# Feature columns transposed two at a time in a recommendation tower, and a last duo in which four late features are worked apart from the others

## What is computed

```python
e = jnp.stack([tbl_f[ids[:, f]] for f in range(26)], axis=1)
combined = jnp.concatenate([dense_output[:, None, :], e], axis=1)       # B, 27, 128
interactions = jnp.einsum('bfd,bgd->bfg', combined, combined)
z = jnp.concatenate([dense_output, interactions[:, iu, ju]], axis=1)    # iu, ju: upper triangle, k=1
h = jnp.concatenate([z, r_dense_output], axis=1)
h = jnp.maximum(h @ W_top1 + b_top1, 0.0)     # 607 -> 512
h = jnp.maximum(h @ W_top2 + b_top2, 0.0)     # 512 -> 256
y = h @ W_top3                                # 256 -> 1
```

## Time and profile before

| what | value |
|---|---|
| runs | median 523.08 us of 3 (521.77 to 524.66) |
| the profiled execution | 513.81 us, of which the span of its instructions is 512.0 us |
| granted TensorE clock, mean | 0.917 of full speed |
| PE busy | 408.9 us, 4352 matmul instructions |
| DVE, ACT, POOL busy | 245.8, 136.1 and 263.1 us |

### The profile page before, as it was taken

The page is one execution under the profiler, slowest core; times in us unless marked ns, Lnnn a source line. Parts: engine busy times, 40 slices in busy tenths (PEclk is TensorE's granted clock), DMA queues, the critical chain, the costliest instruction groups (busy, mean ns, idle before and its releaser), DMA issues.

```text
span 512.0 us, 10047 instructions
## 1 busy us (share of the span) xinstructions
PE 408.9 (80%) x4352; PEld 362.6 (71%) x4352; DVE 245.8 (48%) x312; ACT 136.1 (27%) x356; POOL 263.1 (51%) x280
## 2 busy tenths in 40 slices
PE   2885387857979688879878799797887968887998
PEld 2664366746867578768867678686776857886976
DVE  5994127554445454446453454545543454433332
ACT  2451112321223222223212322233212222123531
POOL 6787464552556636454635646264463654635000
PEclk9997596978999799998989979898998979989999
DMA  7978112221212212221212212123121221211000
GB/s 197 249 187 258 36 47 67 70 67 42 63 42 86 84 33 65 61 87 49 68 43 72 73 53 68 37 83 83 49 57 52 70 65 49 57 32 53 3 12 1
DMA packets 20133, 36.74 MB, mean 72 GB/s; under 512 B 6157, under 2 KB 9877, under 8 KB 20090
## 3 DMA queue, kind: packets, MB, share of 16 engines
q0 software_dynamic: 8704, 17.84, 12.7%
q1 hardware_dynamic: 5338, 9.08, 6.8%
q10 hardware_dynamic: 6048, 9.18, 5.9%
HBM read 36.07 MB, written 0.01 MB: 70 GB/s over the span
## 4 chain that ended last, share of the span: by engine, by line
PE 61%; another core or an unknown queue 13%; issue 12%; DVE 10%; ACT 2%; DMA 1%; SPq 0%; ACTq 0%; DVEq 0%
PE psB L382 23%; PE psG L408 14%; DVE one_hot L646 7%; PE psB L453 7%; PE psB L366 5%; PE psB L460 4%; PE psB L418 2%; PE psB L447 2%; DVE tab_lo L651 2%; PE psB L432 2%; DMA ET<-tbl 1%; PE psB L465 1%; DVE ZH L510 1%; ACT ET L553 1%
## 5 line engine op out<-in xcount | busy, mean ns | idle before, releaser
L307 POOL DMA_INDIRECT E<-tbl,gidx x272 | 262.3, 964 | 206.7 <-PE psB L366 109.7
L646 DVE TENSOR_TENSOR one_hot<-oidx,psR 125x1024 fp32r<-125x1024 int32 (+1 forms) x152 | 179.2, 1189 | 116.3 <-remote 60.4
L382 PE MATMUL psB<-one_hot,tab_hi 125*128 125x256 f32 x592 | 117.9, 321 | 19.0 <-ACT tab_hi L535 9.4
L408 PE MATMUL psG<-ET 128*52 128x52 f32 x2048 | 81.9, 228 | 44.4 <-issue 35.7
L382 PE MATMUL psB<-one_hot,tab_lo 125*128 125x256 f32 x592 | 105.4, 302 | 5.6 <-issue 4.7
L408 PEld LDWEIGHTS psG<-ET 128*52 128x52 f32 x2048 | 67.8, 139 | 59.2 <-issue 54.5
L382 PEld LDWEIGHTS psB<-one_hot,tab_hi 125*128 125x128 f32 x592 | 88.4, 206 | 27.3 <-issue 20.5
L382 PEld LDWEIGHTS psB<-one_hot,tab_lo 125*128 125x128 f32 x592 | 90.1, 208 | 9.1 <-issue 7.5
L669 DVE COPY_PREDICATED S<-second,psG 116x208 f32<-116x208 int32 x64 | 25.0, 391 | 103.1 <-ACT S L582 94.0
L582 ACT COPY S<-psG 116x208 f32<-116x208 f32 x64 | 21.2, 333 | 146.6 <-remote 82.0
L553 ACT COPY ET<-psB 128x512 f32<-128x512 f32 (+3 forms) x80 | 44.3, 572 | 50.9 <-PE psB L366 30.9
(11 more groups left out here) (46 smaller groups left out, 188.7 us busy)
## 6 DMA issues: line engine op xcount, KB each, us to landing
oidx<-hot_idx ACTq DMA_DIRECT2D x28, 256.0 KB
E<-tbl,gidx POOLq DMA_INDIRECT x272
ET<-tbl SPq DMA_DIRECT2D x3, 448.0 KB
oidx<-hot_idx SPq DMA_DIRECT2D x4, 256.0 KB
dense<-dense_pairs SPq DMA_DIRECT2D x8, 128.0 KB
ZH<-tbl SPq DMA_DIRECT2D x2, 448.0 KB
S<-tbl SPq DMA_DIRECT2D x2, 448.0 KB
oidx<-hot_idx ACTq DMA_DIRECT2D x7, 128.0 KB
```

The costliest lines, as they stand in the source:

```text
L307: nc.gpsimd.indirect_dma_start(E[:, n % SLOTS, i, :], None, gathered[feature_and_tile(n, i)[0]], bass.IndirectOffsetOnAxis(ap=gidx[:, 4 * ...
L382: product = nc.tensor.matmul(bank[:, t % 2 * DUO:(t % 2 + 1) * DUO], tab[0:ROWS_P, TABLE_BASE[t] + k0 + i, :], one_hot[0:ROWS_P, m % RING, ...
L408: gram = nc.tensor.matmul(psG[g % 2][q * LANE:q * LANE + M, a * M:(a + 1) * M], two[:, 0:M], two[:, PAIR:], start=True, stop=True)
L646: nc.vector.tensor_tensor(one_hot[0:ROWS_P, m % RING, 0:many], ids, rows, ALU.is_equal).then_inc(hot_full[m % RING], 1)
```

## The change

- Column transposes: `S` is laid out [.., duo parity, feature, 64], so that two neighbouring features lie side by side, and one transpose turns both: 13 for each duo, in four `C` steps (0 to 3, 4 to 7, 8 to 10 and 11 to 12 of the 13 twos) instead of 26 in seven. The even feature of a two lands on partitions 0 to 63, the odd one on 64 to 127.
- `U` has 128 partitions and 4 x 256 values. The first 128 columns (twos 0 to 10 but for two 5) hold both sides. The other 128 hold two 5 and the last two twos, one side in the first 64 columns on the lower partitions, the other in the last 64 on the upper ones; the rest stays zero. It is cleared once, in half 2.
- The splits are two: split 0 is four transposes of [128, 128]; split 1 is four float32 matmuls of `U` with `stacked`, two identity matrices one above the other, which brings the two halves together. ACT and DVE make high and low parts of 512 and of 256 values.
- The order of features becomes small tables first, gathered ones last, and the rows of W1 are permuted with it on the host.
- The last duo: T67 brings the last four features of the last tile. Its grams for that tile leave them out (44 columns instead of 52). A new step `late` computes them for all 32 sample groups (64 float32 matmuls with 8 moving columns) into one `psG` bank. The steps of half 16 are: gram, gram, last part of duo 6, gram, gram, C0, C1, C2, T67, split 0, late, first 0, C3, first 1, split 1, first 2, first 3, parts. `first` is the dense products and the first two thirds of the pairs of a first-layer block; its part then has only the last 3 products. In half 15 the order is grams, T64, parts, T65, parts 2 to 5 of duo 6, T66.

```diff
+    LATE = 4
+    TWOS = (F - 1) // 2
+    EARLY = TWOS - LATE // 2
+    COLUMNS = [range(t, min(t + 4, EARLY)) for t in range(0, EARLY, 4)] + [range(EARLY, TWOS)]
+    FIRST_BLOCKS = [(0, 1), (1, 2), (2, 4), (4, 5), (6, 8), (8, 10), (10, 11)]
+    LAST_BLOCKS = [(11, 13), (5, 6)]
...
-            rest = parts(DUOS - 2)[M1:]
-            return (rest[:1] + grams[:2] + rest[1:2] + grams[2:] + rest[2:] + columns(DUOS - 1) +
-                    splits(DUOS - 1) + parts(DUOS - 1))
+            d, turned = DUOS - 1, columns(DUOS - 1)
+            return (grams[:2] + parts(d - 1)[-1:] + grams[2:] + turned[:-1] + [("T", T_GROUPS - 1)] +
+                    splits(d)[:1] + [("late", d)] + firsts(d)[:1] + turned[-1:] + firsts(d)[1:2] + splits(d)[1:] +
+                    firsts(d)[2:] + parts(d))
...
+        if h == TILES - 1:
+            return spread(turns[:-2], steps + after) + parts(d - 1)[M1:-1] + turns[-2:-1]
...
-        S = sb("S", [P, F - 1, 2, DUO_J], f32)
+        S = sb("S", [P, 2, F - 1, DUO_J], f32)
...
-                        gram = nc.tensor.matmul(psG[g % 2][q * LANE:q * LANE + M, a * M:(a + 1) * M],
-                                                two[:, 0:M], two[:, PAIR:], start=True, stop=True)
+                        gram = nc.tensor.matmul(psG[g % 2][q * LANE:q * LANE + many, a * many:(a + 1) * many],
+                                                two[:, 0:many], two[:, PAIR:PAIR + many], start=True, stop=True)
...
+            def late_fill(d):
+                g, tile, many = LATE_FILL, 2 * d + 1, PAIR * LATE
+                wait_out(pe, ("T", T_GROUPS - 1))
+                pe.wait_ge(G_out[g % 2], g // 2)
+                for j in range(TILE_J):
+                    for q in range(GROUP // PAIR):
+                        two = ET[:, tile % ET_RING, j, q].rearrange("p f s -> p (f s)")
+                        gram = nc.tensor.matmul(psG[g % 2][q * LANE:q * LANE + M, j * many:(j + 1) * many],
+                                                two[:, 0:M], two[:, PAIR * F - many:], start=True, stop=True)
                 gram.then_inc(G_full[g % 2], 1)
...
+                if d == DUOS - 1 and b == len(COLUMNS) - 1:
+                    pe.wait_ge(G_out[LATE_FILL % 2], LATE_FILL // 2 + 1)
                 bank, full = wait_empty(pe, ("C", d, b))
-                for i, c in enumerate(COLUMNS[b]):
-                    turned = nc.tensor.transpose(bank[0:DUO_J, i * P:i * P + MT], S[0:MT, c - 1, d % 2, :],
-                                                 ident[0:MT, 0:MT])
+                for i, t in enumerate(COLUMNS[b]):
+                    two = S[0:MT, d % 2, 2 * t:2 * t + 2, :].rearrange("p f j -> p (f j)")
+                    turned = nc.tensor.transpose(bank[:, i * P:i * P + MT], two, ident[0:MT, 0:MT])
...
-            def turn_pairs(d, kp):
-                if kp == 0:
-                    last = {}
-                    for b in range(len(COLUMNS)):
-                        bank, used, _ = PLACE["C", d, b]
-                        last[bank] = used + 1
-                    for bank, count in last.items():
-                        pe.wait_ge(bank_out[bank], count)
+            def turn_pairs(d, i):
+                last = {}
+                for b in range(len(COLUMNS))[:-1] if i == 0 else range(len(COLUMNS))[-1:]:
+                    bank, used, _ = PLACE["C", d, b]
+                    last[bank] = used + 1
+                for bank, count in last.items():
+                    pe.wait_ge(bank_out[bank], count)
+                bank, full = wait_empty(pe, ("split", d, i))
                 for v in range(GROUP):
-                    turned = nc.tensor.transpose(bank[:, v * DUO_J:(v + 1) * DUO_J],
-                                                 U[0:DUO_J, v, kp * P:(kp + 1) * P], ident[0:DUO_J, 0:DUO_J])
+                    if i == 0:
+                        turned = nc.tensor.transpose(bank[:, v * P:(v + 1) * P], U[:, v, 0:P], ident[:, :])
+                        continue
+                    turned = nc.tensor.matmul(bank[:, v * DUO_J:(v + 1) * DUO_J], U[:, v, P:], stacked[:, :],
+                                              start=True, stop=True)
...
+            def copy(sides, low, high, base):
+                at, n = low - COLUMNS[b][0], high - low
+                turned = bank[sides, at * P:(at + n) * P].rearrange(
+                    "p (t h f s) -> p h s t f", t=n, h=2, s=PAIR)[:, :, :, :, 0:2 * high]
+                rows = U[sides, :, base:base + n * 2 * high].rearrange("p (h s) (t f) -> p h s t f", h=2, t=n)
+                return nc.scalar.copy(rows, turned) if eng is nc.scalar else nc.vector.tensor_copy(rows, turned)
+            for low, high in FIRST_BLOCKS:
+                if low in COLUMNS[b]:
+                    copied = copy(slice(0, P), low, high, block_base[low, high])
+            for low, high in LAST_BLOCKS:
+                if low in COLUMNS[b]:
+                    copy(slice(0, DUO_J), low, high, block_base[low, high])
+                    copied = copy(slice(DUO_J, P), low, high, block_base[low, high] + DUO_J)
...
-                    act.wait_ge(w1d_lo_ready, 1)
-                    act.wait_ge(w1_lo_ready, 1)
+                    act.wait_ge(U_cleared, 1)
...
+                dve.wait_ge(w1_lo_ready, 1)
+                dve.wait_ge(w1d_lo_ready, 1)
+                nc.vector.memset(U[:, :, :], 0.0).then_inc(U_cleared, 1)
+                dve.wait_ge(U_cleared, 1)
```

More of the change, by code:

```diff
@@ L83, in splits, with firsts @@
     def splits(d):
-        return [("split", d, kp) for kp in range(KP)]
+        return [("split", d, i) for i in range(2)]
     def parts(d):
         return [("part", d, p) for p in range(PARTS)]
+    def firsts(d):
+        return [("first", d, p) for p in range(M1)]
     HALVES = range(2 * DUOS + 1)
@@ L145, in place_fills @@
         for i, step in enumerate(STEPS):
-            if step[0] == "gram" or (step[0] == "hot" and step[2] not in FILL_FIRST):
+            if step[0] in ("gram", "late") or step in places or (step[0] == "hot" and step[2] not in FILL_FIRST):
                 continue
+            if step[0] == "first":
+                step = ("part", *step[1:])
             bank = min(range(BANKS), key=lambda x: ended[x])
@@ L165, in gram_number @@
         return d * G_FILLS + i
+    LATE_FILL = DUOS * G_FILLS
     def chunk_number(d, c):
@@ new lines, in pair_products, with first_products @@
+            def pair_products(d, p, bank, kp):
+                cols = slice(p * P, (p + 1) * P)
+                if p == 0:
+                    wait_out(pe, ("split", d, kp // 2))
+                for w, z in ((w1p_hi, Zp_hi), (w1p_hi, Zp_lo), (w1p_lo, Zp_hi)):
+                    layer = nc.tensor.matmul(bank[:, 0:DUO], w[:, kp, cols], z[:, kp, :],
+                                             start=False, stop=(kp == KP - 1 and w is w1p_lo))
+                return layer
+            def first_products(d, p, bank):
+                cols = slice(p * P, (p + 1) * P)
+                if p == 0:
+                    pe.wait_ge(Zd_lo_ready, d + 1)
+                for w, z in ((w1d_hi, Zd_hi), (w1d_hi, Zd_lo), (w1d_lo, Zd_hi)):
+                    nc.tensor.matmul(bank[:, 0:DUO], w[:, cols], z[:, :],
+                                     start=(w is w1d_hi and z is Zd_hi), stop=False)
+                for kp in range(KP - 1):
+                    pair_products(d, p, bank, kp)
@@ L439, in written, with begin_part @@
+            def begin_part(d, p):
+                bank, _ = wait_empty(pe, ("part", d, p))
+                first_products(d, p, bank)
+            def perceptron_part(d, p):
+                if p < M1 and d == DUOS - 1:
+                    bank = psB[PLACE["part", d, p][0]]
+                    full = bank_full[PLACE["part", d, p][0]]
+                else:
+                    bank, full = wait_empty(pe, ("part", d, p))
                 def written(other):
@@ L442, in perceptron_part @@
                 if p < M1:
[L443 to L454 removed]
+                    if d < DUOS - 1:
+                        first_products(d, p, bank)
+                    layer = pair_products(d, p, bank, KP - 1)
                 elif p < M1 + M2:
@@ L573, in empty_hot @@
                     copied = nc.scalar.copy(
-                        features(2 * d + half, 1 + NG + first, many),
+                        features(2 * d + half, 1 + first, many),
                         psB[bank][:, 0:many * DUO].rearrange(
@@ L624, in _ @@
                         empty_gram_first(step[1], step[2])
+                    elif step[0] == "late":
+                        empty_late_first(step[1])
                     elif step[0] == "C" and on_scalar(step[2]):
@@ L707, in _ @@
                         empty_gram(step[1], step[2])
+                    elif step[0] == "late":
+                        empty_late(step[1])
                     elif step[0] == "C" and not on_scalar(step[2]):
@@ L739 @@
```

(22 more changed lines are left out.)

119 lines of the change are left out of this document (67 added, 52 removed).

## The result

The changed kernel took 530.86 us (median of 20 runs, 523.53 to 538.71), the kernel before 522.35 (20 runs, 511.27 to 527.58). Executions of one kernel scatter by 1% and more, so every ratio with an interval leaves out the runs that lie over 1.5% above the fastest of their kernel. Here it is **1.023, 95% interval 1.017 to 1.030: slower by 2.3%**. The prediction was 517.5, faster, with a range to 526.0. The profiled execution of the changed kernel took 535.97 us and is one of its longer ones, while that of the kernel before, 513.81, is one of its shorter ones; so the 22 us between the two traces overstate the difference, and places are read from them, not sizes.

The account below looks back on a forecast made before the run. PE's order of work was taken to bound the kernel. Columns and splits -8.6, clearing U +0.7, code -0.7 and the last duo +3.0 summed to -5.6 us: 523.1 to 517.5 us, range from near 509.5 to 526.

Parts of the forecast that it names:

- What bounds the kernel: Whole kernel: PE's order of work paces the gathers; PE lacks time to pauses in grams and column-step holds; last gather not awaited.
- Columns and splits, -8.6 us: Duos 0 to 6: fewer column and split transposes save 1.23 us per duo, full credit for seven, -8.6 us.
- Clearing U, +0.7: Half 2: a DVE memset of some 0.95 us delays the first gram copies, 0.3 us slack, +0.7 us.
- Code, -0.7: PE's instruction stream: 26 fewer of 1,088 instructions per duo shorten gram pauses if those are instruction fetches, -0.7 us in seven.
- The last duo, +3.0: Tail: late step +3.4, two new waits +0.9 each, savings in columns, grams and a split wait; sum +3.0 us.
- Rival 3: In front of split 0: waits gather, the clock falls behind them; slower, +8.4 us, 531.5 us; chance 0.10.
- My "against it": Split 0: objection to waits gathering there, that DVE's 2.1 us fit under PE's 2.5.
- Rival 1: Column stage: the saving hides beside pauses and holds, a quarter of the credit left; +0.8, 523.9 us, no change; chance 0.22.
- Rival 2: Column stage: most of PE's 11.0 us wait for DVE's copies before column transposes goes; -13.6, 509.5 us; chance 0.15.
- Rival 4: Last duo: late grams cost 74 ns each, +6.1 on the sum; 523.6 us, no change; chance 0.08.

Follow-up runs that it names:

- group 4: Runs on one chip with pauses: kernel before 520.2 us, changed kernel 1.011, kernel before with new hot-step places 1.019; both without gathers 378.5 and 379.3 us.
- Group 2: Runs on a chip without pauses: kernel before 384.7 us, changed kernel 385.7; with gathers replaced by one clearing of the slots, 379.0 and 378.9 us.
- group 3: Runs on a chip without pauses: kernel before 384.7 us, changed kernel 1.0044; changed kernel with the last duo's former order and no late step 0.990.
- old tail and old places: Changed kernel with halves 15 and 16 ordered as before, no late step, hot steps where they stood before: 1.002 against the kernel before (525.9 us).
- putting the columns early: Changed kernel with duos 0 to 6's column steps ahead of the last second-layer part and third layer: 1.031 against the kernel before, 552.6 us.

## Why the prediction was wrong

**What bounds the kernel.** Right that PE paces, that the last gather isn't waited for, and that pauses and the hold in the column stage are what PE lacks. Wrong was to leave both as a fixed surrounding: the sum has no term for the new places of the hot and gathered steps. With what the clock loses behind them they are 142 of the 520 us on the chip of group 4, they lie where POOL's gathers run together, and POOL's runs follow PE's gathered steps, whose transposes free the slots. An edit that moves these steps moves the gathers and the pauses with them. The trace had the hint: the pauses fall together with runs of POOL, and the tail, where POOL is silent, has none.

**Columns and splits, -8.6 us.** This is the step that failed in the sum: full credit of 1.23 us for each of seven duos. Without gathers, the time from one third-layer step to the next went from 43.71, 44.14, 43.72, 44.14 and 43.72 us to 43.18, 44.01, 43.18, 44.01 and 43.18: **-0.37 us a duo, not -1.23**, about -2.6 in seven. Two terms were mis-sized. The stacked matmuls take 118 ns (0.94 us) to 137 ns (1.10 us in the chain of duo 3), above even my upper bound of 110, where I had taken 74 from the nearest transpose; that is +0.35 to +0.5. And PE waits 0.3 us at each of the two splits of the duo shown (+0.6), where I had none: I compared DVE's 2.1 us with PE's 2.5 for split 0 alone; split 1 also needs C3's two copies of 0.37 us, 2.65 us of DVE in all, from the one-hot tile's start to the end of the six copies. Where no such wait stands, in duo 6, the same steps save 0.8. The wide transposes, 92 ns for 105, cost no more than I took.

**Clearing U, +0.7.** PE waits 2.23 us for the gram copies in half 2 instead of 0.83: +1.4. The memset took 912 ns, as estimated; the slack of 0.3 us that I read at 89.85 to 90.59 belonged to a kernel with pauses. And I had no term for the clock: behind the longer wait it is granted at 0.50 from 64 to 66 us, in both traces of the changed kernel without gathers, and the four steps there take 4.4 us instead of 3.0, +1.4 again. The stretch from there to duo 1's first gram, with duo 0's column stage in it, then gains 2.1 us, 0.8 of it a wait that is gone in front of the splits, so that +0.8 is left.

**Code, -0.7.** No run tests a share for PE's code. Nothing supports it: where gathers are left out the same code runs without a pause, and the instruction queue moved 35 packets with pauses as without. The Trainium skill's statement that fetching is mostly hidden (Runtime: NRT & Kernel Launch, Instruction fetch mechanics), which I had argued against, agrees with the runs without gathers, in which PE's longest unexplained wait after half 2 in the kernel before is under 0.2 us. The pauses are no price of code alone; whether gathers slow the fetching was not tested.

**The last duo, +3.0.** Right, term by term: 36.3 us from its first gram to the end before, 39.2 after without gathers in group 4 (+2.9). The late step took 3.19 to 3.47 us for 3.4, 25 to 27 ns an instruction; the two new waits 0.84 and 0.84 for 0.9 and 0.9. What the sum lacks is the clock. In three of the eight traces that have a late step, that of the result among them, it fell to its lower level right behind it, without idle time of PE, and the tail was 1.5 us longer. Group 2's changed kernel without gathers (us; busy us of PE, PEld, DVE, ACT, POOL; clock; DMA share, GB/s):

```profile
364.00:366.00 2.00, 2.00 (x11) 2.00 (x10) 0.30 (x1) 0.27 (x1) 0.00 (x0) 0.50 0.00 0
```

With gathers, on a chip without pauses, the tail costs 4.6 us (group 3); the profiled execution there has no such fall, and no run explains the rest.

**What is beyond the sum.** In the two traces of group 4 without gathers the stretches add up to what the span grew: +0.8 up to duo 1's first gram, -1.9 from the third layer of duo 0 to that of duo 5, -0.8 for duo 6's column stage, +2.9 for the last duo, +1.0 us in all (the two steps that moved ahead of the third layer, 1.4 us, cancel). By the medians, without gathers, the change measured -0.1 and +0.8, with them on a chip without pauses +1.0 and +0.5 us. On the chip of the result it lost 8.5. The new places of the hot and gathered steps by themselves cost 1.9% (1.3 to 2.5) and 3.7% on two chips with pauses, and taking them and the tail back leaves 0.2% (-0.3 to +0.8) on a third. So the places are shown to be enough for a loss of this kind. What in them does it is open. One candidate: after 150 us POOL has two runs of twelve gathers in the trace before and four in the trace after, all over a column stage (a run here may have breaks of up to 1.3 us); but the kernel with the old tail and old places, which loses nothing, has three, over column stages too. And the terms don't add up neatly, since on one chip the whole change lost less (1.1%) than the places alone (1.9%), though their intervals overlap.

**The rivals.** Rival 3 had the sign and, at 531.5, the number, and the number is luck. Waits in front of split 0 longer than 2.91 us are in the trace (3.01, 5.17 and 4.40), with the lower clock behind them. But putting the columns early took them away and didn't cure the loss, the duo with 4.40 us is no longer than before, and the kernel with the longest holds loses nothing that can be measured. My "against it" held, but for 0.3 us, where there are no pauses. Rival 1 named a quarter of the credit; without gathers 30% of it is there (0.37 of 1.23), but not for its reason, since no hold is left to hide the saving. With pauses the duos got longer, which it doesn't explain. Rival 2 is wrong: PE's waits in front of column steps did fall, from 19.3 us to 6.3, but 19.4 us now stand in front of the splits, where there were 3.2. Rival 4 is wrong: a late instruction took 25 to 27 ns, not 74.

## What to carry to other kernels

Before work is priced by its spacing, ask whether the pauses around it belong to the code or to what another engine does at the time; a kernel variant without that traffic, or a run on a second chip, tells. When a list of steps is mixed by weights, a change in the number of steps moves everything that is mixed with it: keep the places fixed when the content is to be compared. A copy chain must be summed up to the last reader, not to the first. A wait that grows is priced with what the clock does behind it.

## What was not expected of the hardware

- The same kernel took 385 us on two chips and 520 to 535 on four (medians of the kernel before). With its indirect gathers left out it took 378.4 to 379.0 us on either kind. Which property of the chip or its surroundings decides is open; so is the mechanism by which gathers hold up PE, and the signals to ACT and DVE.
- On a chip with pauses, half of the gathers, nearly all in runs of two (2.2 us), left 388.7 us; all of them, in runs of four and more, 525.9. The pauses start 2.5 us into a run, in the trace with all of them and in that with half. Whether all 272 gathers, issued two at a time with a break of some us, would run near 390 us on such chips wasn't tried; it would be the first thing to try, as it is worth over 100 us where this change was about 5.
- Where a chip has no pauses, 270 gathers in one unbroken run, from 3.4 to 351 us, do PE no such harm: from 123 to 351 us it is busy all the time at a clock of 1.00 (group 2).
- The clock can fall to its lower level behind 128 short matmuls (8 moving columns) without any idle time of PE; it did in three traces of eight, and no run tells what decides.
